# Turning two tiles in a row in every second step of a three-layer graph network kernel

## The reference, cut to what matters

```python
def _sage_conv(x, src, dst, Wp, bp, Wl, bl, Wr):
    h = jax.nn.relu(x @ Wp.T + bp)
    agg = jax.ops.segment_sum(h[src], dst, num_segments=N)
    cnt = jax.ops.segment_sum(jnp.ones((src.shape[0],), x.dtype), dst, num_segments=N)
    agg = agg / jnp.maximum(cnt, 1.0)[:, None]
    return agg @ Wl.T + bl + x @ Wr.T
...
h = jnp.maximum(_layernorm(x, axis=-1), 0.0)
# layer 0 and 1: _sage_conv, then relu and a layer norm with gain and shift; layer 2: _sage_conv
x = x + _L0_gnn_ref(h, edge_index, ...)
```

## Time and profile before

| | us |
|---|---|
| runs of the kernel | 1567.98, 1569.55, 1569.79 |
| median | 1569.55 |
| the profiled execution: its own time | 1569.72 |
| its span in the trace | 1568.0 |
| PE busy within the span | 1526.6 |
| DVE, ACT, POOL busy | 973.0, 718.5, 563.1 |
[...]

### The profile page before, as it was taken

The page is one execution under the profiler, slowest core; times in us unless marked ns, Lnnn a source line. Parts: engine busy times, 40 slices in busy tenths (PEclk is TensorE's granted clock), DMA queues, the critical chain, the costliest instruction groups (busy, mean ns, idle before and its releaser), DMA issues.

```text
span 1568.0 us, 21733 instructions
## 1 busy us (share of the span) xinstructions
PE 1526.6 (97%) x7518; PEld 1247.8 (80%) x7518; DVE 973.0 (62%) x2158; ACT 718.5 (46%) x1366; POOL 563.1 (36%) x529
## 2 busy tenths in 40 slices
PE   5999999999999999999999999999999998999996
PEld 4777888788888788888878888878888886788885
DVE  6877786655555576777565555557666665555552
ACT  5767543232333576776323232357576652232321
POOL 4655435344422100100334442324353465344323
PEclk9999999999999999999999999999999999999998
DMA  9887775455454787888645555479999985455434
GB/s 312 299 289 235 242 257 188 128 88 93 89 88 61 190 276 257 287 266 276 204 107 93 88 90 91 55 227 318 317 325 328 326 287 174 75 87 90 72 48 54
DMA packets 150604, 289.12 MB, mean 184 GB/s; under 512 B 18456, under 2 KB 18496, under 8 KB 150496
## 3 DMA queue, kind: packets, MB, share of 16 engines
q1 hardware_dynamic: 123616, 224.81, 42.5%
q0 software_dynamic: 26880, 62.93, 23.0%
HBM read 130.89 MB, written 156.78 MB: 183 GB/s over the span
## 4 chain that ended last, share of the span: by engine, by line
PE 93%; DVE 3%; ACT 1%; DMA 1%; POOL 1%; issue 1%; POOLq 0%; SPq 0%; ACTq 0%
PE bank L685 14%; PE bank L686 14%; PE bank L684 14%; PE bank L672 10%; PE bank L818 7%; PE bank L820 7%; PE bank L819 7%; PE bank L797 6%; PE bank L798 6%; PE bank L799 6%; DVE h_pre L1247 1%; DMA out<-rows_out,into_i 1%; PE bank L733 1%; DVE h_low L1253 1%; ACT h_high L949 0%
## 5 line engine op out<-in xcount | busy, mean ns | idle before, releaser
L684 PE MATMUL bank<-w_high,h_low 128*128 128x512 f32 x900 | 375.1, 417 | 0.0
L685 PE MATMUL bank<-w_low,h_high 128*128 128x512 f32 x900 | 358.7, 399 | 0.0
L686 PE MATMUL bank<-w_high,h_high 128*128 128x512 f32 x900 | 357.0, 397 | 0.0
L949 ACT ACTIVATE h_high<-h_pre 128x500 fp32r<-128x500 f32 x120 | 74.7, 622 | 457.5 <-DVE h_pre L1247 457.5
L567 POOL DMA_INDIRECT rows_in<-node_x,sorted_src x120 | 117.0, 975 | 310.5 <-PE bank L672 243.0
L686 PEld LDWEIGHTS bank<-w_high,h_high 128*128 128x128 f32 x900 | 170.6, 190 | 39.1
L818 PE MATMUL bank<-w_high,h_low 128*125 128x512 f32 x480 | 192.1, 400 | 8.0 <-DVE h_low L1253 8.0
L684 PEld LDWEIGHTS bank<-w_high,h_low 128*128 128x128 f32 x900 | 171.2, 190 | 31.1
L685 PEld LDWEIGHTS bank<-w_low,h_high 128*128 128x128 f32 x900 | 171.5, 191 | 30.7
L1039 DVE TENSOR_TENSOR h_low<-bank,h_high 128x512 fp32r<-128x512 f32 x152 | 105.1, 692 | 146.0 <-ACT h_high L895 143.2
L797 PE MATMUL bank<-xt_low,w_high 128*128 128x500 f32 x480 | 195.1, 406 | 0.0
(11 more groups left out here) (131 smaller groups left out, 2296.1 us busy)
## 6 DMA issues: line engine op xcount, KB each, us to landing
node_x<-xn SPq DMA_DIRECT2D x237, 256.0 KB, 3.3
rows_in<-node_z SPq DMA_DIRECT2D x158, 256.0 KB, 4.2
node_z<-rows_out SPq DMA_DIRECT2D x142, 256.0 KB, 2.1
out<-rows_out SPq DMA_DIRECT2D x79, 256.0 KB, 3.2
rows_in<-x SPq DMA_DIRECT2D x78, 256.0 KB, 3.6
residual<-x SPq DMA_DIRECT2D x78, 256.0 KB, 4.0
node_z<-bias_z SPq DMA_DIRECT2D x16, 256.0 KB, 3.6
rows_in<-node_x SPq DMA_DIRECT2D x16, 256.0 KB, 2.7
```

The source lines that it names most:

```text
L684: nc.tensor.matmul(psum, low[:, k, :], w_high("r", l)[:, k, :], start=(k == 0), stop=False)
L685: nc.tensor.matmul(psum, high[:, k, :], w_low("r", l)[:, k, :], start=False, stop=False)
L686: last = nc.tensor.matmul(psum, high[:, k, :], w_high("r", l)[:, k, :], start=False, stop=(k == K - 1))
```

## The change

Node phase: in an even step i, tiles i+2 and i+3 are turned one behind the other, and in an odd step none. This goes for PE's transposes, ACT's high parts and DVE's low parts alike. Edge phase: in an even step s, edge tiles s+8 and s+9 are turned, and in an odd step none. The ring of turned node tiles gets a fourth place, which lies in a free third chunk of the first halves of `h_high` and `h_low`; ACT's wait for the last node product moves from group 1 to group 0, where those halves are written. The layout of the late tiles stays as it was under the name `XT_HOME`. No instruction is added or removed; only their order changes, and the late tiles' order does not.

```diff
-XT_RING = 3
+XT_RING = 4
+XT_HOME = 3
...
         def node_xt(high, t):
 
-            return by_chunk(flat(h_high if high else h_low, 1), t % XT_RING)
+            h, s = h_high if high else h_low, t % XT_RING
+            return by_chunk(flat(h, 1 - s // XT_HOME), s if s < XT_HOME else XT_HOME - 1)
...
+        def node_turns(l, i):
+
+            return [t for t in (i + AHEAD_TURN, i + AHEAD_TURN + 1) if i % 2 == 0 and is_product(l, t)]
+
...
+        def edge_turns_beside(s):
+
+            return [t for t in (s + 2 * GROUP, s + 2 * GROUP + 1) if s % 2 == 0 and t < EDGE_TILES]
...
                 for i in node_steps(l):
-                    if is_product(l, i + AHEAD_TURN):
-                        node_turn(l, i + AHEAD_TURN)
+                    for t in node_turns(l, i):
+                        node_turn(l, t)
...
-                    if s + 2 * GROUP < EDGE_TILES:
-                        edge_turn(l, s + 2 * GROUP)
+                    for t in edge_turns_beside(s):
+                        edge_turn(l, t)
...
-                if g == 1 and m == 0:
+                if g == 0 and m == 0:
                     act.wait_ge(n_product, products_until(l + 1))
...
-                    if is_product(l, i + AHEAD_TURN):
-                        node_xt_high(l, i + AHEAD_TURN)
+                    for t in node_turns(l, i):
+                        node_xt_high(l, t)
...
                 for i in node_steps(l):
-                    if is_product(l, i + AHEAD_TURN):
-                        node_xt_low(l, i + AHEAD_TURN)
+                    for t in node_turns(l, i):
+                        node_xt_low(l, t)
```

More of the change, by code:

```diff
@@ L80, in sage_kernel @@
     assert TABLE_ROWS < P * P and PAIR_ROWS <= 2 * P
-    assert GROUP_ROWS % 2 == 0 and XT_RING * K * P <= K * GROUP_ROWS
+    assert GROUP_ROWS % 2 == 0 and XT_HOME * K * P <= K * GROUP_ROWS
     assert out.shape[0] == TABLE_ROWS and LATE == IN_RING and LATE_TURNS * GROUP == LATE
@@ L373, in node_xt @@
         def node_xt(high, t):
-            return by_chunk(flat(h_high if high else h_low, 1), t % XT_RING)
+            h, s = h_high if high else h_low, t % XT_RING
+            return by_chunk(flat(h, 1 - s // XT_HOME), s if s < XT_HOME else XT_HOME - 1)
         def late_xt(high, j):
             xt, h = (xt_high, h_high) if high else (xt_low, h_low)
-            return by_chunk([xt[0][:], xt[1][:], flat(h, 0)][j // XT_RING], j % XT_RING)
+            return by_chunk([xt[0][:], xt[1][:], flat(h, 0)][j // XT_HOME], j % XT_HOME)
         def edge_xt(buf, t):
@@ L902, in late_xt_high @@
                     act.wait_ge(e_projected, EDGE_TILES * (l + 1))
-                if j == 2 * XT_RING:
+                if j == 2 * XT_HOME:
                     act.wait_ge(e_product, EDGE_TILES * (l + 1) - GROUP)
@@ L1010, in _ @@
                         edge_out(l, s - 1)
-                    if s + 2 * GROUP < EDGE_TILES:
-                        edge_xt_high(l, s + 2 * GROUP)
+                    for t in edge_turns_beside(s):
+                        edge_xt_high(l, t)
                     for j in late_turns(l, s):
@@ L1313, in _ @@
                     g, i = s // GROUP, s % GROUP
-                    if s + 2 * GROUP < EDGE_TILES:
-                        edge_xt_low(l, s + 2 * GROUP)
+                    for t in edge_turns_beside(s):
+                        edge_xt_low(l, t)
                     for j in late_turns(l, s):
```

## The result

The changed kernel takes 1580.26 us (median of 6 runs, 1579.83 to 1581.83), and the kernel before 1568.81 us (6 runs, 1567.11 to 1569.80). The ratio is 1.0075, with a 95% interval from 1.0062 to 1.0088: slower by 0.75%, some 11.5 us. The forecast was 1571.0 with a range to 1578, so the result lies outside it.

What follows compares the result with a forecast made beforehand. PE's own stream was taken to bound the kernel. The terms, +5.0 + 0.4 - 1.9 - 1.3 - 0.4 - 0.5 + 0.2 = +1.5 us, on a median of 1569.55 gave about 1571.0 us, range 1566 to 1578.

Steps and rivals of the forecast that it cites:

- the chain term: Layer 0's first 40 steps: a second DVE subtraction delays `rank`, POOL's masks and the odd `count`; +5.0 us.
- the chain costs more: Rival, slower: POOL's permutation mask takes its long form, 1581, or regular pairs have no margin, 1577.6; chance 0.20.
- turn-to-turn distance: Sign in the changed profile: even steps in layer 0 have 7.5 instead of 7.4 us from turn to turn.
- Turns in pairs: PE in node and edge phases: a pair costs 0.015 less than two single turns, in 127 pairs; -1.9 us.
- Lookups: Ten pairs in steps with lookups: the product following directly on the mask matmul pays a restart; +0.4 us.
- The waits for the low parts: Edge step 0 of each layer: the turn of tile 9 fills PE's wait, three times 0.43; -1.3 us.
- The start: At the kernel's start the third turn moves ahead of PE's 1.0 us wait for a mask; -0.4 us.
- Gathered rows: End of layer 2's node phase: the first gather comes earlier, as step 75 has no subtraction; -0.5 us.
- the second turn's late tile: Layers 1 and 2: PE reaches the second turn before ACT has normalized tile 1; two times 0.1, +0.2 us.
- The two rivals about it: PE's clock stays up, faster, 1565.9, chance 0.12; or falls more often, slower, chance 0.05.
- A change in the number of falls: Sign: the prediction is wrong if PE's clock falls to its lower level a different number of times.
- The prediction's 0.05 for more falls: Rival, slower: PE's clock falls more often, one fall costing 1.7 us; chance 0.05.

Runs made afterwards that it cites:

- run 5: Kernel before with a second subtraction of the same shape added in DVE's even steps of layer 0, its result unread; ratio 1.0043.
- run 3: Changed kernel with DVE's `carry` moved from the odd steps to steps 48 to 67; ratio 1.0030.
- runs 4 and 12: Changed kernel with `rank` of layer 0 at the head of DVE's step, ahead of the low parts, on two chips; ratios 0.9974, then 0.9999.
- run 7: Changed kernel with POOL's permutation masks of layer 0 one step later, behind the count masks; ratio 1.0001.
- run 11: Kernel before, without pairs, with `rank` moved to the head of DVE's step; ratio 0.9997.
- run 9: Kernel before with the ring of four and ACT's moved wait, every tile still turned singly; ratio 1.0004.
- run 6: Kernel before with the ring of four and pairs of node turns in layers 1 and 2 alone; ratio 1.0025.
- run 10: Changed kernel with single node turns in a ring of three, pairs only in the edge phases, on another chip; ratio 0.9987, median 1566.13 us.
- run 8: Changed kernel with DVE's `carry` executed twice, one behind the other; ratio 1.0077.
- run 1: Changed kernel with single node turns in a ring of three, pairs only in the edge phases; ratio 0.9981.

## Why the prediction was wrong

**The step that failed** is the chain term, +5.0, and in it the durations behind `rank`. The forecast moved POOL's masks later by one slot and kept their durations of 0.60; where the mask then would lie in time beside DVE's odd step, which itself moved forward, was not looked at. The rival "the chain costs more" had the right place and kind, POOL's masks getting longer beside DVE's moved work, but named the permutation mask. In these steps that one kept its 0.91, and the count mask behind it grew. Its bound, up to 0.57 more per pair, was too far up. That its 1581 lies so near the measured 1580.26 is luck: it came from another mask and another size.

The size can be taken apart by four pairs of steps, after which the wheel of late tiles repeats. From the odd `count` of step 23 to that of step 31 the profiles show 29.15 us before, 30.16 in run 5, 30.79 in run 3 and 31.81 with the change. So:

| per eight steps | us |
|---|---|
| second subtraction (run 5 less before) | +1.01 |
| `rank` beside the mask (run 3 less run 5) | +0.63 |
| `carry` beside the mask (change less run 3) | +1.02 |
| together | +2.66 |

The forecast had 0.61 + 3 x 0.14 = 1.03 for the first line and nothing for the others. Both halves of its working were thus sound for these steps: no margin in steps with a second tile, 0.47 in regular ones. (The lines are differences between whole kernels, and run 5 differs from run 3 in more than the mask; that the two last lines fit 4 x 0.16 and 4 x 0.26 speaks for the names given to them.) What it lacked is that with the margin used up every further delay is paid in full: 0.42 of mask in each of four pairs are 1.68, and the two last lines together are 1.65. Over 19 pairs the chain costs 12.0 instead of 5.0: 5.95 as in run 5, and 6.05 for the mask. The prediction's turn-to-turn distance, 7.5 instead of 7.4, likewise became 7.95 instead of 7.29 on the average of these eight steps.

Run 5 is 1.0 us above the 5.0. Most of that, 0.7, lies in two pairs near the start, from `count` 7 to `count` 11, which take 7.75 each in it and 7.26 before. The trace of before shows why at `count` 9:

```profile
53.68 0.69 DVE L1028 SCALAR_TENSOR_TENSOR w_low<-stage,w_high 128x512 fp32r<-128x512 f32 x1
53.86 1.28 POOL L609 TENSOR_SCALAR h_pre<-column_no,place 125x250 bf16<-125x250 f32 x1 [1.77 <-DVE unused L1136]
...
55.70 0.60 POOL L600 TENSOR_SCALAR shift_cols<-column_no,lo_f 128x128 bf16<-128x128 f32 x1
...
56.52 0.23 PE L713 MATMUL bank<-shift_cols 128*128 128x128 bf16 x1
```

The permutation mask lies beside an operation of DVE that splits a weight (`w_low`, both inputs in SBUF) and takes 1.28 instead of 0.91. So the margin is 56.52 - 56.30 - 0.06 = 0.16 there and not 0.47, and the second subtraction costs 0.49. The first pair of steps is 0.2 dearer than foreseen too, and I did not follow why.

The same rows say more. The trace of before holds all 38 permutation masks of the earlier trace rows, and their durations fall into four groups: 0.91 with none of DVE's rows on two SBUF inputs beside them, 1.01 with `carry`, 1.28 with `w_low`, and 1.53 with `carry` and `w_low` behind it. The median of 0.958 lies between the first two groups. So that a POOL row grows beside such a row of DVE could have been read ahead of the change, and the step that failed could have been avoided with what was at hand.

**That the chain is the cause** is shown by two cuts at different links, on DVE (runs 4 and 12) and on POOL (run 7). Each leaves pairs and instructions as they are and brings count 39 back to within 0.1 us of before, while the cut without the pairs (run 11) takes off only 0.5 us. Those 0.5 us, 165.8 or 165.9 beside 165.31, are what the pairs themselves cost in these 40 steps once no chain is in the way.

**The mechanism of the long mask** is shown in its outline only. With `rank` ahead of it and `carry` behind `rank`, the mask grows by 0.16 for one and 0.42 for both, and ends 0.39 to 0.47 behind the last row of DVE's unbroken sequence. `rank`, `carry` and `w_low` each have two inputs in SBUF. The output sum reads one of its two from a PSUM bank, and in the changed kernel the permutation mask at 119.48 keeps its 0.91 with such a sum begun 0.18 before it, while the one at 55.85, with `w_low` begun 0.18 before it, takes 1.28. Two inputs in SBUF are not the whole condition: POOL's very first count mask, at 23.90 before and 24.02 after, takes 0.75 beside short conversions of DVE that have one. The order of the two counts as well. With `rank`, whose record starts at 120.76, ahead of the mask at 120.94, the mask grows and `rank` keeps its 0.47. In step 9 of the changed kernel the mask is 0.04 ahead, and it is `rank` that grows:

```profile
57.69 0.60 POOL L610 TENSOR_SCALAR shift_cols<-column_no,lo_f 128x128 bf16<-128x128 f32 x1
57.73 0.60 DVE L1146 SCALAR_TENSOR_TENSOR unused<-dst_row,key_f,ones 125x250 bf16<-125x250 f32 x1
```

The mask does not hold `rank` off for its whole length: this `rank` is over 0.04 behind the mask, though it takes 0.47 alone. Nor does the order of the records explain all. `carry`, at 121.16, keeps its 0.41 although the record of the mask, which grows, had begun at 120.94. With the same two operations the other way round, in run 4, the second one does not keep its time:

```profile
113.85 0.41 DVE L1157 TENSOR_TENSOR carry<-dst_row 128x249 bf16<-128x249 f32 x1
...
114.03 0.70 POOL L610 TENSOR_SCALAR shift_cols<-column_no,lo_f 128x128 bf16<-128x128 f32 x1
114.18 0.59 DVE L1146 SCALAR_TENSOR_TENSOR unused<-dst_row,key_f,ones 125x250 bf16<-125x250 f32 x1
```

The mask takes 0.70 here and `rank` 0.59. The record's start may not be the start of its reading; that was not tried, and what decides between the two cases is open.

**Turns in pairs, -1.9 predicted.** The term had the wrong sign. Three pairs of turns in layer 2 of the changed kernel:

```profile
1200.91 1.04 PE L682 MATMUL bank<-ident,xn 128*128 128x128 f32 x8
...
1201.70 0.47 PE L694 MATMUL bank<-w_high,h_low 128*128 128x512 f32 x1
1202.02 0.39 PE L695 MATMUL bank<-w_low,h_high 128*128 128x512 f32 x1
...
1207.38 1.03 PE L682 MATMUL bank<-ident,xn 128*128 128x128 f32 x8
...
1213.85 1.04 PE L682 MATMUL bank<-ident,xn 128*128 128x128 f32 x8
```

A pair takes 0.79 to the next matmul, as in the earlier trace rows. But two steps take 6.47, and the kernel before needs two times 3.22:

```profile
1289.28 0.60 PE L672 MATMUL bank<-ident,xn 128*128 128x128 f32 x4
...
1292.50 0.60 PE L672 MATMUL bank<-ident,xn 128*128 128x128 f32 x4
1295.72 0.60 PE L672 MATMUL bank<-ident,xn 128*128 128x128 f32 x4
```

So a pair costs 0.03 more, where 0.015 less was forecast. The turns did save their 0.02. But the starts of the product's matmuls, averaged over some 500 distances in layer 2, lie 233.0 ns apart with pairs, 231.3 before and 231.5 in run 9, which has the ring of four and single turns; over the 24 matmuls of two steps the 1.7 ns make 0.04 us. In layer 0's first 40 steps they stood about 233 ns apart already. Why they do is open. Run 6 says with its 1.0025 (2.5 to 5.5 us) that pairs in the upper layers cost more than the some 2 us which this distance and the starts of the layers account for. The rest goes with the granted clock. Four of its ten runs had a mean granted clock of 0.991 and took 1571.2 us on average, 1.7 more than the 1569.5 of the kernel before at that clock. The other six had 0.990, which none of the 20 runs of the kernel before beside them had. Why they were granted less is open.

**The smaller terms.** Lookups: +0.6 in steps 48 to 67, of +0.4 foreseen (product 47 is over 12.0 us later than before and product 67 12.6 later); of it some 0.2 is the slower spacing, which sets in there too. The waits for the low parts: 2.02 us instead of the 2.46 in the earlier trace rows, three times -0.44, of -0.43 foreseen. The stretch of the changed kernel (columns as in the earlier trace rows):

```profile
303.04:305.06 2.02, 0.00 (x1) 0.00 (x0) 1.33 (x3) 1.38 (x3) 0.00 (x0) 1.00 0.63 187
```

The start: the wait for a mask shrank from 0.99 to 0.35, and `count` 1 comes 0.25 earlier (28.39, before 28.64), of -0.4 foreseen. Gathered rows: the wait is 2.8 instead of 3.3 in the lists, of -0.5 foreseen. Layers 1 and 2: +1.1 and +1.2, growing evenly by 0.03 from pair to pair. The dearer pairs (35 and 39 times 0.03) make nearly all of it, so that next to nothing is left for the +0.1 each that the second turn's late tile was to cost. The edge phases run 0.1, 0.3 and 0.4 faster beyond the waits and the clock, and what follows the last product is 0.4 shorter. The list of waits has one more line that the earlier trace rows leave out, 3.1 us of PE at the third turn for the low part of the first tile, and it is 3.2 after the change.

**The sum** of what was seen: +12.0 in layer 0's first 40 steps (the start among it), +0.6 in its later steps, +2.3 in the node phases of layers 1 and 2, -1.3 and -0.5 in the waits, -0.8 in the edge phases, -0.4 behind the last product, and -1.7 for one fall of the clock fewer. That is +10.2, and the spans differ by 10.1. So the terms other than the chain, -3.5 in the forecast, came to -1.9.

**The clock.** The two rivals about it played no part in the loss; the mean granted clock was 0.991 before and 0.992 after. After the wait in layer 0, where the clock was 0.50 for 3.40 us in the earlier trace rows, it stays up in the changed kernel:

```profile
305.06:308.46 3.40, 3.40 (x15) 2.75 (x16) 2.97 (x4) 0.56 (x2) 0.00 (x0) 1.00 0.00 0
```

Fifteen matmul records fit where ten did, since behind the first of them they start 0.22 to 0.24 apart, where before, at the clock of 0.50, it was 0.41 to 0.43; that is roughly the 1.7 us put on a fall. Between the first products and the last, the clock of before falls to its lower level six times for 3.4 us, and in the changed kernel the time at that level is that of five such falls (one is twice as long). A change in the number of falls was one of the prediction's signs of being wrong; it came, as one fall fewer. That may be chance: run 6, whose layer 0 is that of the kernel before, has none after the wait in layer 0 either. The prediction's 0.05 for more falls was the author's estimate: no run shows that turns in a row beside a wait bring the clock down. The four profiles with single turns throughout (before, runs 5, 9 and 11) have the time of five or six such falls, and the ten with pairs that of three to six.

The edge pairs (run 10) show what the falls do to a timing. Their profiled execution had three and took 1562.43; the eleven runs reach from 1562.38, at a mean granted clock of 0.995, to 1569.48, at 0.990. The kernel before ran at 0.991 or 0.992 beside them. At 0.992 it took 1567.7 us on average (21 runs) and the edge pairs 1565.9 (2 runs); at 0.991 it took 1569.3 (12 runs) and the edge pairs 1567.2 (1 run). So the clock makes most of the spread, while the gain of some 2 us is there at equal clock too, though on few runs.

## What to carry to other kernels

A chain that arrives just in time does not stand in the list of waits: look for a matmul that starts 0.06 us behind the last thing it needs, and price every later arrival at that place in full, times the number of rounds. When a change moves work on two engines in opposite directions, lay their new times side by side and see what comes to lie beside what; an instruction's duration from the old profile may hold only beside the old neighbours (here a count mask of 0.60 came to take 1.02). And if two steps' work is put in one, put what others wait for ahead of it (`rank` here): with that order the same pairs cost nothing that the ratio could show, though they still brought nothing.

## What the runs showed of the hardware

A mask of POOL that began 0.11 to 0.19 us after a DVE row on two SBUF inputs took longer, in the kernel before too (of the 38 permutation masks those without such a row took 0.91, the others 1.01, 1.28 or 1.53). A POOL instruction of 0.60 us on 128 x 128 numbers took 0.76 when `rank`, a DVE instruction that reads two SBUF operands, had begun 0.18 before it, and 1.02 when `carry` followed `rank` without a pause; with `carry` first and `rank` behind it, it took 0.70. DVE's row grew too: `rank`, 0.47 alone, took 0.60 when the mask had begun 0.04 before it and 0.59 behind `carry` in run 4. After a pause of 0.04 us between DVE's instructions (121.57 to 121.61 in run 8) POOL finished 0.39 later, while DVE's next instruction ran its 0.42.

On the chip of runs 1 to 4 the kernel before took 1573.78 us, and 1568.07 and 1568.12 on the chips of the others. Ratios of that chip came out lower than on the later ones (0.9974 and 0.9999 for run 4's kernel, 0.9981 and 0.9987 for run 1's), so the sizes above are taken from the times of `count` in the profiles, which repeat within 0.1 us. The profiles of that chip also show short stops of PE ahead of a turn that nothing in the trace ends, here in the list of PE's waits of run 4:

```profile
PE bank L682 <- issue: 1.1, 2, 0.6
```

The cause is not known.
